# Attention of a graph layer: pairs of heads in plain float32 on halves of the array, two steps to a turn

## The chip, the cores and the metric

One core of one Trainium2 chip. The metric is the device time of one launch in microseconds (us). TensorE multiplies matrices, VectorE, ScalarE and GpSimd work on elements, SyncE (SP) issues most transfers. PSUM, which TensorE writes, has eight banks here, `bank[0]` to `bank[7]`, each of 128 partitions x 512 float32.

## The reference, cut to what matters

```python
xn = layernorm(x)                                   # 1250 x 512
neigh = segment_sum(xn[src], dst)                   # 40000 edges
rst = (1 + eps) * xn + neigh
gnn = relu(rst @ W1 + b1) @ W2 + b2 + xn            # hidden 1024
q, k, v = split(xn @ W_qkv.T)                       # 8 heads of 64
attn = relu((q * 64**-0.5) @ k.T) @ v               # per head, no softmax
x = x + gnn + attn @ W_out.T + b_out
x = x + moe(layernorm(x))                           # 16 experts, top 2, hidden 256
```

## The kernel before

All work is ordered by hand: each engine has its own list of instructions, and counting semaphores tie them together. One arena in SBUF holds nearly all tensors, which reuse each other's places.

The stages. (1) Layer norm of ten tiles of 128 nodes (the last has 98), turned by TensorE (L1058). (2) Projections k and q by pairs of heads (L1141), 24 groups, then v by tile of nodes (L1152), 10 groups; these 34 "turns" are `NPRE`. (3) Attention. (4) Output projection (L1203). (5) The hidden layer of the graph part (L1272) and its second product (L1218). (6) Routing and the expert loop.

Graph work goes beside (2) and (3). Instead of gathering rows, the kernel counts edges: for each window of 32 target nodes (`w`, 40 of them) VectorE makes pairs of one-hot matrices in float16 from 125 edges (L825, L827) in a ring of `RING` slots, and TensorE multiplies them (L1081), which gives the adjacency counts of the window in PSUM. ScalarE copies the window (L613). After each four windows (group `g`) TensorE multiplies the counts by xn, ten float32 matmuls of 512 columns (`neighbours`, L1110), VectorE adds (1 + eps) xn (L834), TensorE turns the sum (L1117), ScalarE saves it (L618). Where each piece goes is a table: `dve_after`, `pe_after`, `act_after` give for each turn or attention step what an engine does after it. `EVERY` is the number of steps from one window to the next, `start(w)` the step of window w. GpSimd picks the columns of each window's edges (L509, L510) no more than three windows ahead of what VectorE has made.

Attention before runs by single heads. A step is (head, block of 416 or 418 queries, tile of 128 keys): 8 x 3 x 10 = 240 steps. q and k are split into a high part in float32r and a rest, so that float32r products add up to float32 precision. GpSimd splits each head (`split_head`, L494 to L497) on the head's own 64 partitions, and three transfers (L369) copy the parts to the other 64, so that k's high part and rest lie one above the other (`k_hl`). A score tile is then two matmuls over 128 rows, with q's high part and with its rest (L1169). ScalarE makes relu and its float32r rounding `p_hi` (L657), VectorE the rest of it, `p_lo` (L861). v has high and low halves side by side (`v_hl`, L637 and L842), so a value product is again two matmuls (L1185, L1188); its two halves of output partitions are added by ScalarE and VectorE (L646, L854) into q's place. TensorE runs the scores two steps ahead: scores(s + 2), values(s), graph(s). `NQB` = 3 banks hold scores, banks 3 and 4 (`AV`) the values, banks 5 and 7 (`AW`) windows, bank 6 (`NB`) the sums.

v_hl lies over the place of the kept x. So x is fetched again after attention's last step, GpSimd adds xn (L562), and VectorE the biases (L874), before the output projection is added (L876). SP's list in this part: three transfers of a head, one fill of an eighth of the expert slots with zeros (L373), for each head; then w_o; after the last step x, w1, w2.

Of the kernel before, what the change touches and what calls it, by code (L numbers as in the profile page):

```python
# [47 lines left out]
RING = 6  # L48
# [20 lines left out]
def layer(nc, x, src, dst, wqkv, wo, bo, gw1, gb1, gw2, gb2, geps, rw, rb, ew, eb1, eb2, out):  # L69
# [8 lines left out]
    with ExitStack() as ctx:  # L78
# [34 lines left out]
        NPB = 4  # L113
        RSTB = RINGB + 6400
# [4 lines left out]
        zeros = at(RINGB + 10240, [D])  # L119
# [17 lines left out]
        k_hl = [split_tensor(f"k_hl{i}", b, [N]) for i, b in enumerate((SET0, SET1))]  # L137
        q_hi = [split_tensor(f"q_hi{i}", b + 4 * N, [N]) for i, b in enumerate((SET0, SET1))]
        q_lo = [split_tensor(f"q_lo{i}", b + 8 * N, [N]) for i, b in enumerate((SET0, SET1))]
        k_lo = split_tensor("k_lo", TMPK, [N])  # L140
        p_hi = split_tensor("p_hi", PROBS, [NPB, BW])
        p_lo = split_tensor("p_lo", PROBS + NPB * 4 * BW, [NPB, BW])
# [4 lines left out]
        v_hl = split_tensor("v_hl", VT, [NT, HEADS, 2, DH])  # L147
# [9 lines left out]
        def w2_hi(m):  # L157

            return v_hl[:, m // 2, 4 * (m % 2):4 * (m % 2) + 4, :, :].rearrange("p a b c -> p (a b c)")
# [21 lines left out]
        def small(k, *shape):  # L181
# [57 lines left out]
        NQB, AV, AW, NB = 3, 3, (5, 7), 6  # L239
# [4 lines left out]
        x_again = sem("x_again")  # L244
# [18 lines left out]
        qk_ps, p_hi_ready, p_lo_ready, av_step, av_half, av_saved = (  # L263
            sem(s) for s in ("qk_ps", "p_hi_ready", "p_lo_ready", "av_step", "av_half", "av_saved"))
        v_hi_ready, v_lo_ready = sem("v_hi_ready"), sem("v_lo_ready")
        head_split = sem("head_split")
        head_ready = [sem(f"head_ready{h}") for h in range(HEADS)]
# [33 lines left out]
        steps = [(h, b, t) for h in range(HEADS) for b in range(len(BLOCKS)) for t in range(NT)]  # L301
        NS = len(steps)
        SPH = len(BLOCKS) * NT
# [5 lines left out]
        EVERY = 6.7  # L309
        pe_after, act_after, dve_after = ([[] for _ in range(NPRE + NS)] for _ in range(3))  # L310

        def start(w):
            return FROM + w * (NPRE - FROM) / EARLY if w < EARLY else NPRE + (w - EARLY) * EVERY

        for w in range(NW):
            for k in range(USUAL[w]):
                made = int(start(w) + k * (start(w + 1) - start(w)) / USUAL[w])
                dve_after[made].append(("pair", w, k))


                if w % 2 == 0 and k == USUAL[w] - 1:
                    held = ("pair", w, k)
                elif w % 2 == 1 and k == 0:
                    pe_after[made + 1] += [("pair", w, k), ("spare", w - 1), held]
                    act_after[made + (2 if made + 2 < NPRE else 4)].append(("window", w - 1))
                else:
                    pe_after[made + 1].append(("pair", w, k))
            if w % 2 == 1:
                act_after[made + (2 if made + 2 < NPRE else 4)].append(("window", w))
# [11 lines left out]
        def _(sp):  # L341
# [23 lines left out]
            for h in range(HEADS):  # L365
                own, other = slice(DH * (h % 2), DH * (h % 2) + DH), slice(DH - DH * (h % 2), 2 * DH - DH * (h % 2))
# [3 lines left out]
                if h == 0:  # L370
                    sp.wait_ge(zeros_ready, 1)
                fill = FILLS[h]
# [3 lines left out]
            sp.wait_ge(qk_ps, SPH * (HEADS - 1))  # L376
            sp.dma_start(w_o[:, :, :], wo).then_inc(wo_in, 16)
# [48 lines left out]
        def _(pool):  # L426
# [57 lines left out]
            def split_head(h):  # L484

                p, own, i = h // 2, slice(DH * (h % 2), DH * (h % 2) + DH), h % 2
                pool.wait_ge(proj_saved, 6 * (p + 1))
                if h >= 1:
                    pool.wait_ge(head_ready[h - 1], 48)
                if h >= 2:  # L490
                    pool.wait_ge(qk_ps, SPH * (h - 1))
                if h == 1:
                    pool.wait_ge(proj_ps, NPROJ + NT)
                link(pool.tensor_copy(k_hl[i][own, :], k_t[own, p, 0:N]))  # L494
                link(pool.tensor_tensor(k_lo[own, :], k_t[own, p, 0:N], k_hl[i][own, :].bitcast(f32), ALU.subtract))
                link(pool.tensor_copy(q_hi[i][own, :], q_t[own, p, :]))
                link(pool.tensor_tensor(q_lo[i][own, :], q_t[own, p, :], q_hi[i][own, :].bitcast(f32), ALU.subtract))  # L497
                pool.sem_inc(head_split, 1)

# [52 lines left out]

            for _, what, i in sorted([(start(0) + 0.5 if h == 0 else NPRE + SPH * (h - 1) + 1, "head", h) for h in range(HEADS)]
                                     + [(start(max(w - 2, 0)), "cols", w) for w in range(NW)]
                                     + [(start(w), "spare", w) for w in range(0, NW, 2)]):
                {"head": split_head, "cols": window_columns, "spare": spare_chunks}[what](i)
# [34 lines left out]
        def _(act):  # L591
# [43 lines left out]
            for t in range(NT):  # L635
                act.wait_ge(proj_ps, NPROJ + t + 1)
                act.activation(v_hl[:, t, :, 0, :], bank[(NPROJ + t) % 5][:, :].rearrange("p (h d) -> p h d", h=HEADS),  # L637
                               copy).then_inc(v_hi_ready, 1)
                graph(NPROJ + t)

            def save_attention(m):

                h, b = m // 3, m % 3
                o, n = BLOCKS[b]
                act.wait_ge(av_step, NT * (m + 1))
                act.activation(q_t[DH * (h % 2):DH * (h % 2) + DH, h // 2, o:o + n], bank[AV + m % 2][0:DH, 0:n],  # L646
                               copy).then_inc(av_half, 1)

            for s, (h, b, t) in enumerate(steps):
# [5 lines left out]
                if s == 0:  # L655
                    act.wait_ge(proj_ps, NPRE)
                act.activation(p_hi[0:kt, s % NPB, 0:n], bank[s % NQB][0:kt, 0:n], ACT.Relu).then_inc(p_hi_ready, 1)  # L657
                if s > NT and s % NT == 1:
                    save_attention(s // NT - 1)
                graph(NPRE + s)  # L660
            save_attention(HEADS * 3 - 1)
# [9 lines left out]
            for f, tiles in enumerate(FC_TILES):  # L671
# [3 lines left out]
                for m in range(KH):  # L675
                    if tiles[0] == 0:
                        act.activation(w2_hi(m), w2[:, m, :], copy).then_inc(w2_hi_ready, 1)
# [46 lines left out]
        def _(dve):  # L724
# [113 lines left out]
            for turn in range(FROM, NPRE):  # L838
                if turn >= NPROJ:
                    t = turn - NPROJ  # L840
                    dve.wait_ge(v_hi_ready, t + 1)
                    dve.tensor_tensor(v_hl[:, t, :, 1, :],  # L842
                                      bank[turn % 5][:, :].rearrange("p (h d) -> p h d", h=HEADS),
                                      v_hl[:, t, :, 0, :].bitcast(f32), ALU.subtract).then_inc(v_lo_ready, 1)
# [3 lines left out]
            def add_attention(m):  # L848

                h, b = m // 3, m % 3  # L850
                o, n = BLOCKS[b]
                to = q_t[DH * (h % 2):DH * (h % 2) + DH, h // 2, o:o + n]
                dve.wait_ge(av_half, m + 1)
                dve.tensor_tensor(to, to, bank[AV + m % 2][DH:P, 0:n], ALU.add).then_inc(av_saved, 1)  # L854

            for s, (h, b, t) in enumerate(steps):
                n = BLOCKS[b][1]
                kt = rows(t)
                dve.wait_ge(p_hi_ready, s + 1)

                dve.scalar_tensor_tensor(out=p_lo[0:kt, s % NPB, 0:n], in0=bank[s % NQB][0:kt, 0:n], scalar=0.0,  # L861
# [519 lines left out]
```

## Time and profile before

| | us |
|---|---|
| median of 3 runs | 878.91 (877.94 to 879.23) |
| the profiled execution's own time | 879.67 |
| its span | 877.5 |
| PE busy in the span | 775.1 (88%) |
| DVE (VectorE) busy | 521.7 (59%) |
| ACT (ScalarE) busy | 281.1 (32%) |
| POOL (GpSimd) busy | 155.3 (18%) |

PE is TensorE's matmuls, PEld its weight loads. A record's duration runs until its result is out; records in a row begin before the last one ends, so the cost of a matmul in a row is the time from start to start. Each plain float32 matmul shows as two records, each with a load; a float32r or float16 one as one record. PEclk is the granted TensorE clock, 1.00 for 2.4 GHz and 0.50 for 1.2 GHz. Shapes in a row are partitions x elements.

### The profile page before, as it was taken

What the parts mean: (1) busy time and instruction counts of PE and PEld (TensorE: products, weight loads), DVE (VectorE), ACT (ScalarE), POOL (GpSimd) and SP (SyncE); (2) the same over time, 40 slices, a digit from 0 to 9 for tenths busy, and PEclk for the clock granted to TensorE, in tenths of its full rate; (3) what the DMA queues carried; (4) which work ended last, traced back from release to release, by engine and by line L of the source; (5) the groups of instructions that cost most, each with busy time, mean ns of one, the idle gap of its engine ahead of it and who ended that gap; (6) DMA issues with size and microseconds to landing.
All of it is one profiled execution on the core that took longest, in us unless ns stands there. A gap on an engine that the chain in (4) does not pass through costs nothing.

```text
span 877.5 us, 11469 instructions
## 1 busy us (share of the span) xinstructions
PE 775.1 (88%) x3351; PEld 517.9 (59%) x3352; DVE 521.7 (59%) x1494; ACT 281.1 (32%) x578; POOL 155.3 (18%) x198
## 2 busy tenths in 40 slices
PE   4999998989989998979799999999998599999910
PEld 2555443666756676656577744677887256766700
DVE  4563336798989989898877534435445523333234
ACT  2212111352534444343345402323333123434300
POOL 5040003022130403040400042002021100000045
PEclk9999999999999999999799999999999559999965
DMA  9126000807162526253351091001015945343357
GB/s 296 8 44 241 1 0 1 295 1 251 46 210 87 182 104 198 98 160 137 105 191 49 1 357 47 1 0 72 1 73 192 377 184 187 109 135 114 131 163 235
DMA packets 48071, 111.61 MB, mean 127 GB/s; under 512 B 7066, under 2 KB 7082, under 8 KB 45584
## 3 DMA queue, kind: packets, MB, share of 16 engines
q1 hardware_dynamic: 43248, 91.41, 30.8%
q0 software_dynamic: 3616, 11.17, 4.0%
q10 hardware_dynamic: 1152, 8.39, 2.4%
q8 instruction: 24, 0.39, 0.2%
q14 instruction: 31, 0.25, 0.1%
HBM read 44.73 MB, written 58.54 MB: 118 GB/s over the span
## 4 chain that ended last, share of the span: by engine, by line
PE 70%; DVE 20%; issue 4%; POOL 2%; DMA 2%; ACT 2%; SPq 0%; DVEq 0%; POOLq 0%
PE bank L1110 8%; PE bank L1141 7%; PE bank L1272 7%; DVE arena L825 6%; PE bank L1218 6%; PE bank L1333 6%; PE bank L1169 6%; DVE p_lo L861 6%; PE bank L1346 5%; PE bank L1081 4%; PE bank L1152 4%; PE bank L1203 4%; DVE arena L827 3%; PE bank L1188 3%; PE bank L1185 3%
## 5 line engine op out<-in xcount | busy, mean ns | idle before, releaser
L657 ACT ACTIVATE p_hi<-bank 128x416 fp32r<-128x416 f32 (+1 forms) x240 | 123.8, 518 | 201.2 <-PE bank L1169 199.7
L861 DVE SCALAR_TENSOR_TENSOR p_lo<-bank,p_hi 128x416 fp32r<-128x416 f32 (+1 forms) x240 | 140.2, 586 | 40.7 <-ACT p_hi L657 39.7
L825 DVE TENSOR_SCALAR arena<-iota,arena 125x128 f16<-125x128 f16 x392 | 137.9, 352 | 37.0 <-PE bank L1081 34.8
L827 DVE TENSOR_SCALAR arena<-iota,arena 125x320 f16<-125x320 f16 x392 | 115.7, 295 | 0.0
L1169 PE MATMUL bank<-q_hi,k_hl 128*128 128x416 f32 (+1 forms) x240 | 114.9, 479 | 0.1
L1188 PE MATMUL bank<-p_lo,v_hl 128*128 128x416 f32 (+1 forms) x240 | 91.0, 379 | 21.6 <-DVE p_lo L861 21.2
L1110 PE MATMUL bank<-arena 128*128 128x512 f32 x200 | 103.0, 597 | 0.8 <-ACT arena L618 0.8
L1081 PE MATMUL bank<-arena 125*128 125x320 f16 x392 | 96.7, 311 | 5.8 <-issue 3.5
L1185 PE MATMUL bank<-p_hi,v_hl 128*128 128x416 f32 (+1 forms) x240 | 86.5, 360 | 0.0
L1169 PE MATMUL bank<-q_lo,k_hl 128*128 128x416 f32 (+1 forms) x240 | 86.1, 359 | 0.0
L1081 PEld LDWEIGHTS bank<-arena 125*128 125x128 f16 x392 | 34.4, 100 | 75.7 <-issue 53.2
L1141 PE MATMUL bank<-arena 128*128 128x416 f32 (+1 forms) x192 | 73.1, 529 | 2.1 <-ACT arena L600 2.1
L1272 PE MATMUL bank<-arena 128*128 128x384 f32 (+2 forms) x256 | 70.3, 430 | 0.0
L1188 PEld LDWEIGHTS bank<-p_lo,v_hl 128*128 128x128 f32 x240 | 46.6, 194 | 35.2 <-DVE p_lo L861 34.1
L1333 PEld LDWEIGHTS bank<-arena 128*128 128x128 f32 x448 | 53.0, 198 | 17.4 <-issue 16.0
L1333 PE MATMUL bank<-arena 128*128 128x128 f32 x448 | 55.3, 283 | 6.6 <-issue 5.6
L1026 DVE COPY arena<-arena 128x1024 f32 x30 | 20.8, 695 | 67.3 <-issue 67.3
L1169 PEld LDWEIGHTS bank<-q_hi,k_hl 128*128 128x128 f32 x240 | 47.1, 196 | 20.2 <-issue 13.5
L1272 PEld LDWEIGHTS bank<-arena 128*128 128x128 f32 x256 | 47.7, 190 | 17.6 <-issue 0.5
L1141 PEld LDWEIGHTS bank<-arena 128*128 128x128 f32 x192 | 36.2, 195 | 29.7 <-issue 26.3
L509 POOL COPY arena<-arena 125x20 f32 (+1 forms) x40 | 8.5, 212 | 246.8 <-DVE arena L827 207.5
L1346 PE MATMUL bank<-arena 128*128 x112 | 50.4, 592 | 0.0
(208 smaller groups left out, 1018.9 us busy)
## 6 DMA issues: line engine op xcount, KB each, us to landing
slots<-arena SPq DMA_DIRECT2D x6, 5376.0 KB, 19.3
slots<-arena SPq DMA_DIRECT2D x2, 5120.0 KB, 19.0
arena<-in_ew SPq DMA_DIRECT2D x8, 1024.0 KB, 10.7
arena<-in_ew ACTq DMA_DIRECT2D x8, 1024.0 KB, 13.2
arena<-slots SPq DMA_DIRECT2D x32, 256.0 KB, 2.8
slots<-arena SPq DMA_DIRECT2D x28, 256.0 KB, 2.1
arena<-in_gw SPq DMA_DIRECT2D x2, 2048.0 KB, 16.7
arena<-in_wqkv SPq DMA_DIRECT2D x3, 1024.0 KB, 14.2
```

The lines of the kernel that those rows point to most:

```text
L657: act.activation(p_hi[0:kt, s % NPB, 0:n], bank[s % NQB][0:kt, 0:n], ACT.Relu).then_inc(p_hi_ready, 1)
L825: dve.tensor_scalar(ring[:, at_slot:at_slot + P], iota16[0:CE, 0:P], window_cols[:, i % WBUF, 1, k:k + 1], None, ALU.is_equal)
L827: dve.tensor_scalar(ring[:, at_slot + P:at_slot + OHW], iota16[0:CE, :], window_cols[:, i % WBUF, 0, k:k + 1], None, ALU.is_equal).then_in ...
L861: dve.scalar_tensor_tensor(out=p_lo[0:kt, s % NPB, 0:n], in0=bank[s % NQB][0:kt, 0:n], scalar=0.0, in1=p_hi[0:kt, s % NPB, 0:n].bitcast(f3 ...
L1081: return pe.matmul(bank[AW[w % 2]][:, 0:WCOL], of[:, at_slot:at_slot + P], of[:, at_slot + P:at_slot + OHW], start=start, stop=stop, skip_ ...
L1110: ins = pe.matmul(bank[NB][:, :], a_t[:, g % 2, t, :], xn[:, t, :], start=(t == 0), stop=(t == NT - 1))
L1141: ins = pe.matmul(bank[g % 5][:, 0:n], w_qkv[:, k, c:c + P], xn_t[:, k, o:o + n], start=(k == 0), stop=(k == KD - 1))
L1169: ins = pe.matmul(bank[s % NQB][0:kt, 0:n], k_hl[h % 2][:, t * P:t * P + kt], q[h % 2][:, o:o + n], start=first, stop=not first)
L1185: pe.matmul(bank[AV + m % 2][:, 0:n], v_hl[0:kt, t, h, :, :], p_hi[0:kt, s % NPB, 0:n], start=(t == 0), stop=False)
L1188: pe.matmul(bank[AV + m % 2][:, 0:n], v_hl[0:kt, t, h, :, :], p_lo[0:kt, s % NPB, 0:n], start=False, stop=(t == NT - 1)).then_inc(av_step, 1)
L1272: ins = pe.matmul(bank[g % 4][:, 0:n], w1[:, k, m * P:(m + 1) * P], rst_t[:, k, o:o + n], start=(k == 0), stop=(k == KD - 1))
L1333: ins = pe.matmul(bank[a][:, m * P:(m + 1) * P], w1_now[:, a, k * DFF + m * P:k * DFF + m * P + P], xg_t[:, a, k, :], start=(k == 0), stop ...
```

## The change

Attention runs by pairs of heads in plain float32. Nothing is split any more: head 2p lies on partitions 0 to 63 and head 2p + 1 on 64 to 127 of q_t and k_t as the projections leave them. A step is (pair, block, tile of keys), 120 in all. Its scores are two float32 matmuls of 64 rows, one on the upper and one on the lower half of the array's rows, into two banks. ScalarE makes relu of the first head, VectorE of the second, both in float32. Its values are two float32 matmuls over 128 rows, each on one half of the array's columns, into the two halves of one bank, which ScalarE saves in one copy. Two steps make a turn: TensorE does the scores of both, then the graph work of both, then the values of both. Probabilities have two buffers instead of four, values one bank instead of two. A window comes every 3.35 steps, a one-hot pair is used two steps after it is made, the ring has eight slots, and the sums go two to a step. v_sb has half of v_hl's size, so x stays where it is: it isn't fetched again, and GpSimd adds xn and the biases as soon as its list reaches them. w_o and w2 are fetched at attention's start.

```diff
-RING = 6
+RING = 8
-        NPB = 4
+        NPB = 2
+        probs = at(PROBS, [NPB, 2, BW])
-        v_hl = split_tensor("v_hl", VT, [NT, HEADS, 2, DH])
+        v_sb = at(VT, [NT, D])
+        w2_hi = split_tensor("w2_hi", VT, [KH, D])
-        NQB, AV, AW, NB = 3, 3, (5, 7), 6
+        AV, AW, NB = 4, (5, 7), 6
-        steps = [(h, b, t) for h in range(HEADS) for b in range(len(BLOCKS)) for t in range(NT)]
+        steps = [(p, b, t) for p in range(PAIRS) for b in range(len(BLOCKS)) for t in range(NT)]
-        EVERY = 6.7
+        EVERY = 3.35
+        def used(made):
+            return made + (2 if made >= NPRE - 1 else 1)
...
-                    pe_after[made + 5 + t].append(("sum", g, t))
-                dve_after[made + NT + 6].append(("sum", g))
-                pe_after[made + NT + 7].append(("turn", g))
-                act_after[made + NT + 10].append(("turn", g))
+                    pe_after[used(made) + 3 + t // 2].append(("sum", g, t))
+                dve_after[used(made) + 8].append(("sum", g))
+                pe_after[used(made) + 11].append(("turn", g))
+                act_after[used(made) + 12].append(("turn", g))
...
-            for h in range(HEADS):
...
-                sp.wait_ge(head_split, h + 1)
-                for to, of in ((k_hl[h % 2], k_lo), (q_hi[h % 2], q_hi[h % 2]), (q_lo[h % 2], q_lo[h % 2])):
-                    sp.dma_start(to[other, :].bitcast(f32), of[own, :].bitcast(f32)).then_inc(head_ready[h], 16)
+            sp.wait_ge(zeros_ready, 1)
+            for i, fill in enumerate(FILLS):
+                sp.wait_ge(qk_ps, 1 + i * NS // len(FILLS))
...
+                if i == 0:
+                    sp.dma_start(w_o[:, :, :], wo).then_inc(wo_in, 16)
+                    sp.dma_start(w2[:, :, :], gw2).then_inc(w2_in, 16)
...
             sp.wait_ge(av_step, NS)
-            sp.dma_start(xr[:, 0:9, :], xv).then_inc(x_again, 16)
-            sp.wait_ge(xpad_ready, 2)
-            sp.dma_start(xr[0:LAST, NT - 1, :], x[(NT - 1) * P:N, :]).then_inc(x_again, 16)
             sp.dma_start(w1[:, :, :], gw1).then_inc(w1_in, 16)
-            sp.dma_start(w2[:, :, :], gw2).then_inc(w2_in, 16)
...
-            def split_head(h):
...
-            pool.wait_ge(av_step, NS)
-            link(pool.memset(xr[96:P, NT - 1, :], 0.0))
-            pool.sem_inc(xpad_ready, 1)
-            pool.wait_ge(x_again, 32)
             for t in range(NT):
                 link(pool.tensor_tensor(xr[:, t, :], xr[:, t, :], xn[:, t, :], ALU.add))
+                link(pool.tensor_tensor(xr[:, t, :], xr[:, t, :], bias_b2[:, :], ALU.add))
                 pool.sem_inc(base_ready, 1)
...
+                act.activation(v_sb[:, t, :], bank[(NPROJ + t) % 5][:, :], copy).then_inc(v_saved, 1)
...
+                act.activation(q_t[:, p, o:o + n], bank[AV][:, 0:n], copy).then_inc(av_saved, 1)
...
+                if s >= NT and t == 0:
+                    save_attention(s // NT - 1)
                 act.wait_ge(qk_ps, s + 1)
                 if s >= NPB:
                     act.wait_ge(av_step, s - NPB + 1)
...
+                act.activation(probs[0:kt, s % NPB, 0, 0:n], bank[2 * (s % 2)][0:kt, 0:n],
+                               ACT.Relu).then_inc(p0_ready, 1)
+                if s % 2 == 1:
+                    graph(NPRE + s - 1)
+                    graph(NPRE + s)
...
+                dve.wait_ge(qk_ps, s + 1)
+                if s >= NPB:
+                    dve.wait_ge(av_step, s - NPB + 1)
+                dve.tensor_single_scalar(probs[0:kt, s % NPB, 1, 0:n], bank[2 * (s % 2) + 1][0:kt, 0:n], 0.0,
+                                         op=ALU.max).then_inc(p1_ready, 1)
+                if s % 2 == 1:
+                    for what in dve_after[NPRE + s - 1] + dve_after[NPRE + s]:
+                        do(*what)
...
-                link(dve.tensor_tensor(xr[:, t, :], xr[:, t, :], bias_b2[:, :], ALU.add))
...
             def scores(s):
...
+                if s >= 2:
+                    pe.wait_ge(p0_ready, s - 1)
+                    pe.wait_ge(p1_ready, s - 1)
+                for a in range(2):
+                    ins = pe.matmul(bank[2 * (s % 2) + a][0:kt, 0:n], k_t[DH * a:DH * a + DH, p, t * P:t * P + kt],
+                                    q_t[DH * a:DH * a + DH, p, o:o + n], start=True, stop=True,
+                                    tile_position=(DH * a, 0))
                 ins.then_inc(qk_ps, 1)
+            def values(s):
...
+                if t == 0 and m >= 1:
+                    pe.wait_ge(av_saved, m)
+                pe.wait_ge(p0_ready, s + 1)
+                pe.wait_ge(p1_ready, s + 1)
+                for a in range(2):
+                    h = 2 * p + a
+                    ins = pe.matmul(bank[AV][DH * a:DH * a + DH, 0:n], v_sb[0:kt, t, h * DH:h * DH + DH],
+                                    probs[0:kt, s % NPB, a, 0:n], start=(t == 0), stop=(t == NT - 1),
+                                    tile_position=(0, DH * a), skip_group_check=True)
+                ins.then_inc(av_step, 1)
+
+            for s in range(0, NS, 2):
+                scores(s)
+                scores(s + 1)
                 graph(NPRE + s)
+                graph(NPRE + s + 1)
+                values(s)
+                values(s + 1)
```

## Rows read from the trace of the kernel before

**Rows 1.** By stretch: length, busy PE, PEld, DVE, ACT, POOL, PEclk, DMA share, GB/s.
```profile
146.20:505.00 358.80, 330.81 (x1498) 234.88 (x1499) 307.20 (x904) 149.62 (x306) 70.62 (x86) 0.97 0.39 129
696.00:714.00 18.00, 17.14 (x24) 5.14 (x25) 5.82 (x10) 1.70 (x7) 0.00 (x0) 0.50 0.56 229
```
**Rows 2.** The chain of waits around attention: start us, us, what.
```profile
141.41 3.45 PE bank L1152 x8
...
504.99 34.33 PE bank L1203 x80
539.32 20.64 PE bank L1272 x64
```
**Rows 3.** The chain inside attention, with sums and then without.
```profile
212.64 0.86 PE bank L1110 x2
...
213.64 0.38 PE bank L1169 x2
...
214.21 0.19 PE bank L1188
...
222.54 0.17 DVE arena L825
222.70 0.21 DVE arena L827
222.91 0.50 DVE p_lo L861
```
**Rows 4.** Busy PE and PEld in attention's stretch: L1110, then L1081, then L1117.
```profile
146.20:505.00 358.80, 93.84 (x182) 34.46 (x182) 0.97 0.39 129
146.20:505.00 358.80, 81.94 (x315) 26.96 (x315) 0.97 0.39 129
146.20:505.00 358.80, 5.99 (x40) 4.98 (x40) 0.97 0.39 129
```
**Rows 5.** The chain where eight float32 and two one-hot records follow each other.
```profile
70.46 2.81 PE bank L1141 x8
...
218.93 0.27 PE bank L1081 x2
```
**Rows 6.** Waits in attention's stretch: us in total, times, longest.
```profile
PE bank L1188 <- DVE p_lo L861: 21.2, 17, 3.5
```
**Rows 7.** GpSimd's passes and L825: timeline rows, durations min/median/max, groups.
```profile
245.03 2.88 POOL L497 TENSOR_TENSOR q_lo<-arena,q_hi 64x1250 fp32r<-64x1250 f32 x1
245.63 2.33 DVE L825 TENSOR_SCALAR arena<-iota,arena 125x128 f16<-125x128 f16 x1
...
L825 DVE TENSOR_SCALAR arena<-iota,arena x392: 234/246/2847, 48.1 to 472.4; 125x128 f16<-125x128 f16 x196
...
L495 POOL TENSOR_TENSOR k_lo<-arena,k_hl 64x1250 fp32r<-64x1250 f32 x8 | 23.0, 2880 | 0.7
...
L562 POOL TENSOR_TENSOR arena<-arena 128x512 f32<-128x512 f32 x10 | 16.3, 1634 | 11.8 <-DMA arena<-in_x 10.2 <-POOL arena L562 1.6
```
**Rows 8.** TensorE's timeline from products with 16 rows to turns onto 16 columns.
```profile
701.32 0.33 PEld L1309 LDWEIGHTS bank<-b_sb,arena 16*128 16x128 f32 x1 [0.52 <-issue]
...
703.03 1.91 PE L1309 MATMUL bank<-b_sb,arena 16*128 16x512 f32 x2
704.86 0.10 PEld L1303 LDWEIGHTS bank<-ident,arena 128*16 128x16 f32 x2 [1.50 <-issue]
```
**Rows 9.** Timeline in attention: a first record after a wait, and following ones.
```profile
249.10 0.46 PE L1188 MATMUL bank<-p_lo,v_hl 128*128 128x418 f32 x1 [0.90 <-DVE p_lo L861]
...
246.05 0.35 PE L1169 MATMUL bank<-q_lo,k_hl 128*128 128x418 f32 x1
246.05 0.19 PEld L1185 LDWEIGHTS bank<-p_hi,v_hl 128*128 128x128 f32 x1
```
**Rows 10.** TensorE's timeline where attention begins.
```profile
145.54 0.57 PE L1081 MATMUL bank<-arena 125*128 125x320 f16 x3
146.26 0.19 PEld L1169 LDWEIGHTS bank<-q_hi,k_hl 128*128 128x128 f32 x1 [0.48 <-DVE v_hl L842]
```

More of the change, by code:

```diff
@@ L262, in layer @@
         neigh_ps, rst_ready, rstt_ps, rstt_saved = (sem(s) for s in ("neigh_ps", "rst_ready", "rstt_ps", "rstt_saved"))
[L263 to L267, printed above, removed]
+        qk_ps, p0_ready, p1_ready, av_step, av_saved = (
+            sem(s) for s in ("qk_ps", "p0_ready", "p1_ready", "av_step", "av_saved"))
+        v_saved = sem("v_saved")
         out_ps, out_added = sem("out_ps"), sem("out_added")
@@ L323, in layer @@
                 elif w % 2 == 1 and k == 0:
-                    pe_after[made + 1] += [("pair", w, k), ("spare", w - 1), held]
-                    act_after[made + (2 if made + 2 < NPRE else 4)].append(("window", w - 1))
+                    pe_after[used(made)] += [("pair", w, k), ("spare", w - 1), held]
+                    act_after[used(made) + 1].append(("window", w - 1))
                 else:
-                    pe_after[made + 1].append(("pair", w, k))
+                    pe_after[used(made)].append(("pair", w, k))
             if w % 2 == 1:
-                act_after[made + (2 if made + 2 < NPRE else 4)].append(("window", w))
+                act_after[used(made) + 1].append(("window", w))
             if w % WPG == WPG - 1:
@@ L551, in spare_window @@
                     pool.sem_inc(spare_waited, 1)
-            for _, what, i in sorted([(start(0) + 0.5 if h == 0 else NPRE + SPH * (h - 1) + 1, "head", h) for h in range(HEADS)]
-                                     + [(start(max(w - 2, 0)), "cols", w) for w in range(NW)]
+            for _, what, i in sorted([(start(max(w - 2, 0)), "cols", w) for w in range(NW)]
                                      + [(start(w), "spare", w) for w in range(0, NW, 2)]):
-                {"head": split_head, "cols": window_columns, "spare": spare_chunks}[what](i)
-            pool.wait_ge(av_step, NS)
-            link(pool.memset(xr[96:P, NT - 1, :], 0.0))
-            pool.sem_inc(xpad_ready, 1)
-            pool.wait_ge(x_again, 32)
+                {"cols": window_columns, "spare": spare_chunks}[what](i)
             for t in range(NT):
                 link(pool.tensor_tensor(xr[:, t, :], xr[:, t, :], xn[:, t, :], ALU.add))
+                link(pool.tensor_tensor(xr[:, t, :], xr[:, t, :], bias_b2[:, :], ALU.add))
                 pool.sem_inc(base_ready, 1)
@@ L654, in _ @@
                     act.wait_ge(av_step, s - NPB + 1)
[L655 to L661, printed above, removed]
+                act.activation(probs[0:kt, s % NPB, 0, 0:n], bank[2 * (s % 2)][0:kt, 0:n],
[3 more added lines that the diff above has]
+                    graph(NPRE + s)
+            save_attention(NM - 1)
             def exponents(f):
@@ L676, in _ @@
                     if tiles[0] == 0:
-                        act.activation(w2_hi(m), w2[:, m, :], copy).then_inc(w2_hi_ready, 1)
+                        act.activation(w2_hi[:, m, :], w2[:, m, :], copy).then_inc(w2_hi_ready, 1)
                     act.wait_ge(hid_ps, g + 1)
@@ L838, in _ @@
             for turn in range(FROM, NPRE):
[L839 to L844, printed above, removed]
                 for what in dve_after[turn]:
                     do(*what)
[L848 to L856, printed above, removed]
+            for s, (p, b, t) in enumerate(steps):
                 n = BLOCKS[b][1]
                 kt = rows(t)
-                dve.wait_ge(p_hi_ready, s + 1)
-                dve.scalar_tensor_tensor(out=p_lo[0:kt, s % NPB, 0:n], in0=bank[s % NQB][0:kt, 0:n], scalar=0.0,
-                                         in1=p_hi[0:kt, s % NPB, 0:n].bitcast(f32), op0=ALU.max,
-                                         op1=ALU.subtract).then_inc(p_lo_ready, 1)
-                if s > NT and s % NT == 2:
-                    add_attention(s // NT - 1)
-                for what in dve_after[NPRE + s]:
-                    do(*what)
-            add_attention(HEADS * 3 - 1)
+                dve.wait_ge(qk_ps, s + 1)
[6 more added lines that the diff above has]
+                        do(*what)
             for t in range(NT):
@@ L1155, in _ @@
                 graph(NPROJ + t)
-            pe.wait_ge(v_lo_ready, NT)
+            pe.wait_ge(v_saved, NT)
             def scores(s):
-                h, b, t = steps[s]
+                p, b, t = steps[s]
                 o, n = BLOCKS[b]
                 kt = rows(t)
-                if s >= NQB:
-                    pe.wait_ge(p_lo_ready, s - NQB + 1)
-                if s % SPH == 0:
-                    pe.wait_ge(head_split, h + 1)
-                    pe.wait_ge(head_ready[h], 48)
-                for first, q in ((True, q_hi), (False, q_lo)):
-                    ins = pe.matmul(bank[s % NQB][0:kt, 0:n], k_hl[h % 2][:, t * P:t * P + kt], q[h % 2][:, o:o + n],
-                                    start=first, stop=not first)
-                ins.then_inc(qk_ps, 1)
-            scores(0)
-            scores(1)
-            for s, (h, b, t) in enumerate(steps):
-                if s + 2 < NS:
-                    scores(s + 2)
+                if s >= 2:
[5 more added lines that the diff above has]
+                                    tile_position=(DH * a, 0))
+                ins.then_inc(qk_ps, 1)
+            def values(s):
+                p, b, t = steps[s]
                 n = BLOCKS[b][1]
@@ L1180, in _ @@
                 m = s // NT
-                if t == 0 and m >= 2:
-                    pe.wait_ge(av_saved, m - 1)
-                pe.wait_ge(p_hi_ready, s + 1)
-                pe.matmul(bank[AV + m % 2][:, 0:n], v_hl[0:kt, t, h, :, :], p_hi[0:kt, s % NPB, 0:n],
-                          start=(t == 0), stop=False)
-                pe.wait_ge(p_lo_ready, s + 1)
-                pe.matmul(bank[AV + m % 2][:, 0:n], v_hl[0:kt, t, h, :, :], p_lo[0:kt, s % NPB, 0:n],
-                          start=False, stop=(t == NT - 1)).then_inc(av_step, 1)
+                if t == 0 and m >= 1:
[11 more added lines that the diff above has]
+                scores(s + 1)
                 graph(NPRE + s)
+                graph(NPRE + s + 1)
+                values(s)
+                values(s + 1)
             pe.wait_ge(wo_in, 16)
@@ L1196, in _ @@
                 r = rows(t)
-                pe.wait_ge(av_saved, SPH * HEADS // NT - len(BLOCKS)
-                           + sum(1 for o, n in BLOCKS if o < t * P + r))
+                pe.wait_ge(av_saved, NM - len(BLOCKS) + sum(1 for o, n in BLOCKS if o < t * P + r))
                 if t >= 8:
@@ L1216, in mix @@
                         pe.wait_ge(hid_lo, hidden + m + 1)
[L1217 removed]
+                    for i, (h, w) in enumerate(((h_hi, w2_hi[:, m, :]), (h_lo, w2_hi[:, m, :]), (h_hi, w2_lo[:, m, :]))):
                         ins = pe.matmul(bank[4 + t % 2][0:r, :], h[:, m, c:c + r], w,
```

47 lines of the change are left out of this document (7 added, 40 removed).

## The prediction

> **What bounds the kernel now.** Start with the busy time by stretch [rows 1]: attention, woven with most of the graph work, is the stretch from 146.2 to 505.0 us, 358.8 of the span's 877.5 us. TensorE and VectorE are both near full there (331 and 307 us busy), ScalarE and GpSimd are not. The chain of waits [rows 2] shows what ends last around it: V's projections in front and the output projection behind are dense TensorE work, as 34.33 us from 504.99 and the next line from 539.32 on. So the change is decided inside the stretch.
>
> Inside it, the chain [rows 3] alternates. Where a step carries sums of neighbours it is pure TensorE work: from 212.64 on the chain is two records of L1110 (0.86 us), a one-hot product, and the four fp32r matmuls, 0.38 for the scores' two and 0.19 for each value product. Between the sums the chain goes through VectorE: p_lo 0.50 us, one-hots 0.17 and 0.21.
>
> What TensorE must do there, by start-to-start times rather than by record durations, which overlap: the sums are 182 records [rows 4], and the output projection's 80 records of 512 columns take 34.33 us [rows 2], 0.43 each, so 78.3 us. One-hot products: 315 records [rows 4] at 0.137 (two take 0.27 us [rows 5]), 43.2. Turns of the sums: 40 [rows 4] of 128 columns, at the float32 rate of [rows 5] (2.81 us for 8 x 418 columns) 0.11 each, 4.4. Graph work is 125.9 us. Attention is 960 records of fp32r at 0.188, 180.5. Together 306.4; the other 52.4 us are lost. The granted clock of 0.97 over the stretch means 3% of 359 us, 11 us, at twice that length of half clock; the remaining 41 are waits, mostly for VectorE: TensorE stood 21.2 us before L1188 for p_lo [rows 6], and what longer records hide is not in that. One cause of the late VectorE is visible: a one-hot of L825 lasts 0.25 us in the median and up to 2.85, and the long one in the timeline lies under a GpSimd pass of the head split and ends with it [rows 7]. GpSimd is busy 70.6 us in the stretch [rows 1], most of it with them (L495 alone 23.0 [rows 7]).
>
> **What the change does, part by part.** I count per turn of two steps, 60 turns.
>
> *Matmuls of attention.* Removed: 180.5 us. Added: per step two scores and two value products in plain float32. A plain float32 matmul is two records, and eight records of 418 columns take 2.81 us [rows 5], 0.35 each. So a turn has 8 score records and 8 value records. If nothing runs beside anything: 16 x 0.35 x 60 = 336 us, the upper end. If the halves run side by side perfectly: 168 us, the lower end. No row of this trace shows two matmuls on different halves. I take a staggered overlap: records start in the order of the program (as in all rows here), the two records of one half use the same cells and follow each other, and only the second record of half 0 can lie beside the first of half 1. Eight records then take five slots: 5 x 0.35 = 1.75 us for scores and as much for values, 3.5 per turn, 210 us. That is nearer the lower end; I choose it because the halves share neither rows, bank nor partitions (scores), or columns and partitions (values).
>
> The Trainium skill, "TensorE: Matmul & The Clock Gate", Part 3, holds that matmuls on different parts of the array start some 4 ns apart. No row here shows it; by it with both records side by side the sum would be the lower end, which is in the third rival.
>
> *Going between shapes.* TensorE now goes rows-halved (scores), whole (graph), columns-halved (values), rows-halved again: three changes a turn, 180 in all. The nearest rows are products with 16 rows followed by turns onto 16 columns [rows 8]. Within the run of L1309 a load (701.32) starts while the matmul before it runs. The L1303 load at 704.86 starts only when the last L1309 record, which began about 703.88 (703.03 + 1.91 less its length of 1.06), has streamed its 0.85 us: 0.13 us later, though nothing else held it. At full clock half of that. Then the load itself is exposed: a first record after a wait lasts 0.46 us against 0.35 of a following one [rows 3, 9], 0.11 us. I take 0.2 us a change: 36 us. Below: nothing, if loads go on ahead as they do between fp32r and float32 here. Above: 0.35 (tail of 0.16, load of 0.19), 63 us.
>
> The page "TensorEngine Tiling (Array Packing)", Key Properties, of the Trainium skill says that changing the tiling mode drains the engine. By this rule, the trace agrees: the late load of [rows 8]. It speaks against this change: without it the sum would be 36 us less.
>
> *VectorE and GpSimd.* p_lo (240 x 0.50) becomes 120 reliefs of half 1; add_attention and the lower half of V go; the head splits go, with their DMAs and waits. Per turn VectorE then has 2 x 0.50 (no row shows this operation; L861 of the same shape is the nearest, 0.58 at most) and some 5.9 pairs of one-hots (a window's 392/40 = 9.8 pairs [rows 7] per 3.35 steps) at 0.38, 3.2 us. A turn without sums holds TensorE for 3.5 + 0.6 + 0.8 = 4.9 us, so VectorE is no longer late. The ring of 8 lets one turn's pairs be made while the last turn's are used. ScalarE has half its reliefs. The graph work between scores and values covers both reliefs (0.5 us each); if that cover is gone, in the turns with little of it, at most 0.6 us a turn.
> What comes back: GpSimd's base adds, now 20 passes, are no longer behind attention's end. They start when the last window's columns are done, about step 100 of 120, and last some 20 x 1.63 = 33 us [rows 7]. They can hold L825 as the split did, in the last three windows: before, 70.6 us of GpSimd work went with at most 41 us of waiting; in proportion 19, less because TensorE's turns are longer: 8 us. Clock loss: 4 us instead of 11, since fewer gaps go before it. So 12 us for what is left of 52.4.
>
> *One AV bank.* The first values of a block wait for ScalarE's save of the last. Behind that wait stand values and the next scores, but two scores and the graph work are ahead of it, longer than the 0.52 us copy: nothing. Without this cover 11 x 0.7 = 8 us.
>
> *Order of DMAs, around the stretch.* The fills now wait on scores, w_o and w2 go in early, x isn't fetched again, VectorE's L874 adds go to GpSimd. Nothing of this is on the path: L1203 and L1272 follow attention without a gap [rows 2]; w1 now starts at attention's end and has 34 us. The first scores waited for V's lower half (their load stood 0.48 us [rows 10]); of this the stream of the last one-hot product, three from 145.54 at 0.137, hides all but 0.3 us: -0.3 us.
>
> **Sum.** Stretch after: 125.9 + 210 + 36 + 12 = 383.9 us, against 358.8: +25.1. With -0.3: +24.8. The profiled execution took 879.67 us (its span and 2.2 us around it), so 904.5; the median, 878.91, is 0.8 lower, so by it 903.7: forecast 904 us. Own range 879 to 932 (changes at 0.06 to 0.35 us; the upper end leaves no room for more waits).
>
> **Rivals.**
> *No overlap.* Float32 records on halves run one after another. For: no row shows overlap. Against: the halves share nothing. 336 instead of 210: +126, 1030 us.
> *Overlap held back by loads.* A half's weights are loaded only once the record before it has started, as each load here does [rows 3, 9]. Then a pair of score matmuls takes 0.35 + 0.19 + 0.35 + 0.19 = 1.08 us, and a value pair with 64-column loads (0.14, between 0.10 for 16 columns and 0.19 for 128 [rows 8, 9]) 0.98: 4.12 a turn, 247 us, +37: 941 us.
> *Faster: the changes of shape cost little.* Place: the three borders of each turn. The stretch breaks even where attention's part of a turn is (358.8 + 0.3 - 125.9 - 12)/60 = 3.69 us; five slots twice are 3.5, so below 0.06 us a change the kernel is faster. At nothing: 210 + 125.9 + 12 = 347.9, which is 10.9 less, 868 us. Complete overlap with changes at 0.2 is 168 + 36: 862 us; both, 826. For it: fp32r, float32 and float16 follow each other here without a gap. Against: [rows 8]. I price it at 865.
> *Half clock.* If halves don't keep the granted clock up, TensorE's part of the stretch doubles: 372 more, 1276 us. In 696 to 714 us TensorE is busy with 16-row products at clock 0.50 [rows 1]; but the whole-array work behind it starts at that clock too, so this speaks little for it.
>
> **How the numbers follow.** Staggered overlap 0.38; held by loads 0.14; no overlap 0.26; faster 0.19; half clock 0.03. A difference under 0.2% is what a measurement can't tell from none. The third rival and a thin edge of the forecast give faster 0.20, same 0.04, slower 0.76. The range 850 to 1035 takes in all but half clock, double luck, and no overlap with dearer changes.
>
> **What would show it.** L1110 and L1081 keep their counts. The score and value lines show 480 records each; the chain through a turn gives the slots: 1.75 us for four score matmuls is the forecast, 2.8 no overlap, 1.4 full. At each border the first load starts after the last matmul's stream, or not. VectorE's share falls to about 60%, its L825 is long only near the end. Wrong would be: attention's part of a turn under 3.7 or over 4.5 us, or TensorE waiting for reliefs by more than 10 us in all.

## The result: faster, 848.4 us against 878.4

| | us |
|---|---|
| changed kernel, median of 4 | 848.41 (845.18 to 849.28) |
| kernel before, median of 4 | 878.42 (877.84 to 879.23) |
| ratio, 95% interval | 0.9651 (0.9624 to 0.9678) |
| profiled executions | 848.35 (span 846.6) against 879.67 (877.5) |

The forecast was 904, its range 850 to 1035: wrong in sign, and the result lies just under the range.

The chain of waits of the changed kernel, around attention and in two turns of it (columns as in [rows 2]):

```profile
146.44 1.67 PE bank L1113 x8
...
203.64 1.72 PE bank L1056 x4
205.36 0.41 PE bank L1027 x3
205.77 1.55 PE bank L1130 x8
207.32 1.60 PE bank L1113 x8
208.91 1.91 PE bank L1056 x4
210.83 0.82 PE bank L1027 x6
211.64 1.55 PE bank L1130 x8
213.19 1.60 PE bank L1113 x8
214.79 0.92 PE bank L1027 x6
...
474.07 34.53 PE bank L1152 x80
```

L1113 are the scores, L1130 the values, L1056 the sums (L1110 before), L1027 the one-hot products (L1081), L1152 the output projection (L1203). That projection begins at 474.07 instead of 504.99 [rows 2]: 30.9 us earlier, and the span is 30.9 us shorter. All of the gain is in attention's stretch. There the chain is TensorE alone from attention's start to 404 us, so that VectorE's pieces between the sums [rows 3] are gone; from 404 to 435 us it runs mostly through VectorE's one-hots, which the run late_adds explains below. The stretch by engine (columns as in [rows 1]):

```profile
146.40:474.10 327.70, 323.33 (x1492) 133.43 (x1492) 214.18 (x753) 84.83 (x174) 40.20 (x76) 1.00 0.39 144
```

The granted clock is 1.00 where it was 0.97, VectorE has 214 us of work where it had 307. Eight score records take 1.60 us up to the next work. At 0.35 us a record, eight one after another would be 2.8, and the forecast's five slots 1.75; four slots are 1.40, and the 0.20 left is the border. The timeline shows why: records come in pairs that start within 0.01 us of each other, and so do their loads. The two loads of a pair take 0.14 us together, and the trace has 0.13 to 0.14 for each of them (the first row holds two such pairs, 0.05 us apart):

```profile
205.70 0.20 PEld L1130 LDWEIGHTS bank<-arena 128*64 128x64 f32 x4 [0.26 <-issue]
205.70 1.27 PE L1130 MATMUL bank<-arena 128*64 128x416 f32 x6
...
206.10 0.14 PEld L1130 LDWEIGHTS bank<-arena 128*64 128x64 f32 x2 [0.21 <-issue]
206.45 0.14 PEld L1130 LDWEIGHTS bank<-arena 128*64 128x64 f32 x2 [0.21 <-issue]
```

Six value records last 1.27 us in all, from the first's start to the last's end: three pairs.

What TensorE waits for in the stretch (line, us in total, times, longest) is 4.3 us, against 21.2 for p_lo alone before [rows 6] (L789 and L791 make the two one-hots of a pair, L812 are VectorE's reliefs, L602 is ScalarE's save of V):

```profile
PE bank L1027 <- DVE arena L791: 2.6, 4, 1.1
PE bank L1130 <- DVE arena L812: 1.1, 4, 0.3
PE bank L1027 <- issue: 0.3, 1, 0.3
PE bank L1113 <- ACT arena L602: 0.3, 1, 0.3
```

### The profile page after: what moved, and what is told of

Its sections match the earlier page's. It is cut to its first block, busy times and chain, and to the rows that moved or that the text cites. A ratio compares the mean times of both kernels' runs of the same rounds, so it can differ in the third digit from the quotient of the medians.

```text
span 846.6 us, 11316 instructions
## 1 busy us (share of the span) xinstructions
PE 768.3 (91%) x3351; PEld 417.3 (49%) x3352; DVE 411.5 (49%) x1330; ACT 216.1 (26%) x446; POOL 98.8 (12%) x175
## 4 chain that ended last, share of the span: by engine, by line
PE 84%; DVE 5%; issue 3%; DMA 2%; POOL 2%; SPq 1%; ACT 1%; DVEq 0%; POOLq 0%
PE bank L1113 11%; PE bank L1130 10%; PE bank L1056 10%; PE bank L1087 7%; PE bank L1221 7%; PE bank L1167 7%; PE bank L1282 7%; PE bank L1027 6%; PE bank L1295 6%; PE bank L1098 4%; PE bank L1152 4%; POOL arena L550 2%; PE bank L1258 2%; DMA arena<-in_x 2%; PE bank L1264 1%
## 5 line engine op out<-in xcount | busy, mean ns | idle before, releaser
L789 DVE TENSOR_SCALAR arena<-iota,arena 125x128 f16<-125x128 f16 x392 | 115.9, 296 | 93.2 <-PE bank L1027 91.2
L791 DVE TENSOR_SCALAR arena<-iota,arena 125x320 f16<-125x320 f16 x392 | 117.2, 299 | 0.0
L620 ACT ACTIVATE arena<-bank 128x416 f32<-128x416 f32 (+1 forms) x120 | 62.2, 518 | 200.4 <-PE bank L1113 200.4
L812 DVE TENSOR_SCALAR arena<-bank 128x416 f32<-128x416 f32 (+1 forms) x120 | 70.6, 591 | 80.7 <-PE bank L1113 74.9
L1113 PE MATMUL bank<-arena 64*128 64x416 f32 (+1 forms) x480 | 100.2, 535 | 0.3 <-ACT arena L602 0.3
L1130 PE MATMUL bank<-arena 128*64 128x416 f32 (+1 forms) x480 | 97.2, 525 | 1.3 <-DVE arena L812 1.1
L1056 PE MATMUL bank<-arena 128*128 128x512 f32 x200 | 96.2, 605 | 0.0
L1027 PE MATMUL bank<-arena 125*128 125x320 f16 x392 | 71.2, 300 | 3.0 <-DVE arena L791 2.6
L1113 PEld LDWEIGHTS bank<-arena 64*128 64x128 f32 x480 | 40.6, 183 | 58.2 <-issue 57.6
L1027 PEld LDWEIGHTS bank<-arena 125*128 125x128 f16 x392 | 35.9, 97 | 63.4 <-issue 44.3
L1282 PEld LDWEIGHTS bank<-arena 128*128 128x128 f32 x448 | 53.3, 199 | 17.4 <-issue 15.7
L1221 PEld LDWEIGHTS bank<-arena 128*128 128x128 f32 x256 | 47.7, 190 | 17.6 <-issue 0.5
L1056 PEld LDWEIGHTS bank<-arena 128*128 128x128 f32 x200 | 34.9, 189 | 42.6 <-issue 41.9
L1130 PEld LDWEIGHTS bank<-arena 128*64 128x64 f32 x480 | 29.4, 136 | 43.5 <-issue 36.7
L1087 PEld LDWEIGHTS bank<-arena 128*128 128x128 f32 x192 | 35.7, 193 | 29.9 <-issue 25.4
L534 POOL DMA_INDIRECT slots<-arena,slot x20 | 19.9, 996 | 208.9 <-DVEq L872 204.0
```

What stands on the lines that cost most here:

```text
L620: act.activation(probs[0:kt, s % NPB, 0, 0:n], bank[2 * (s % 2)][0:kt, 0:n], ACT.Relu).then_inc(p0_ready, 1)
L789: dve.tensor_scalar(ring[:, at_slot:at_slot + P], iota16[0:CE, 0:P], window_cols[:, i % WBUF, 1, k:k + 1], None, ALU.is_equal)
L791: dve.tensor_scalar(ring[:, at_slot + P:at_slot + OHW], iota16[0:CE, :], window_cols[:, i % WBUF, 0, k:k + 1], None, ALU.is_equal).then_in ...
L812: dve.tensor_single_scalar(probs[0:kt, s % NPB, 1, 0:n], bank[2 * (s % 2) + 1][0:kt, 0:n], 0.0, op=ALU.max).then_inc(p1_ready, 1)
L1027: return pe.matmul(bank[AW[w % 2]][:, 0:WCOL], of[:, at_slot:at_slot + P], of[:, at_slot + P:at_slot + OHW], start=start, stop=stop, skip_ ...
L1056: ins = pe.matmul(bank[NB][:, :], a_t[:, g % 2, t, :], xn[:, t, :], start=(t == 0), stop=(t == NT - 1))
```

## The experiments

Theory after the result: records on the two halves run side by side in full (168 us of slots); the three changes of shape a turn cost nearly what was forecast; and the larger part of the gain is what the old form lost in waits and half clock, 52.4 us of its stretch. Where a kernel leaves values out, the router sends the rows elsewhere, and the expert loop of 8.5 us a round runs 15 times (one_half) or 13 times (b_no_split, b_both) instead of 14: so I compare where the output projection begins, and give that beside the time. It begins at 505.0 before and 474.1 in the changed kernel.

### One half of the rows for both heads

```diff
-  k_t[DH * a:DH * a + DH, ...], q_t[DH * a:DH * a + DH, ...], tile_position=(DH * a, 0)
+  k_t[0:DH, ...], q_t[0:DH, ...], tile_position=(0, 0)
```

> The changed kernel with both heads' scores on the lower half of the array's rows (head 2p's k and q are used for both heads, so head 2p+1's scores are left out); everything else the same. Theory (records of different halves run side by side, each as long as a whole-array record of as many columns): eight score records a turn take eight slots of 0.35 us instead of four, 60 x 4 x 0.35 = +84 us against the changed kernel's 848, so about 932. Rival (a record on half the array is simply cheap, and side by side explains nothing): no change, 848. Rival (staggered as forecast): from five slots to eight, +63, 911.

Measured 938.6 us (ratio to before 1.068, 1.067 to 1.070); the output projection begins at 555.68, +81.6. The chain:

```profile
203.98 2.99 PE bank L1113 x8
```

2.99 instead of 1.60 for the same eight records: eight slots (2.80) and the same 0.19 at the border. A record on half the array is as long as one on the whole, and the other half is free beside it. Both rivals fall: they expected nothing, and 63 us.

### The two matmuls of one half next to each other

```diff
-                scores(s)
-                scores(s + 1)
+                scores(s, (0,))
+                scores(s + 1, (0,))
+                scores(s, (1,))
+                scores(s + 1, (1,))
```

> The changed kernel with the four score matmuls of a turn in another order: head 2p of both steps, then head 2p+1 of both steps, so that in the program's order the two matmuls of one half stand next to each other. If a record can only start beside its neighbour in the program (strict order of starts), then of four records on one half and four on the other one pair overlaps: seven slots instead of four, +63 us, about 911. If the engine takes whichever half is free, 848 as the changed kernel.

TensorE's wait for the reliefs stands ahead of each step's first matmul, and the semaphore that tells of a step's scores is raised by its second.

Measured 852.0 us (ratio to before 0.969, 0.968 to 0.971), 3.6 over the changed kernel. The chain of this kernel has the same score block:

```profile
208.29 1.60 PE bank L1113 x8
209.89 1.92 PE bank L1056 x4
```

So program order does not set the pairs: TensorE takes the next record of each half, over at least one matmul of the other. The staggered overlap of the forecast assumed the opposite.

The semaphore keeps the order of the program all the same. VectorE's reliefs of one turn in the changed kernel, whose scores begin at 207.25, and of the same turn here, where they begin at 208.22:

```profile
208.26 1.29 DVE L812 TENSOR_SCALAR arena<-bank 128x416 f32<-128x416 f32 x2 [1.89 <-PE bank L1113]
...
209.93 1.09 DVE L812 TENSOR_SCALAR arena<-bank 128x416 f32<-128x416 f32 x2 [2.59 <-PE bank L1113]
```

The first relief starts 1.01 us after the scores in the changed kernel and 1.71 us after them here: the first step is told of only when both steps' matmuls are done (in the median turn the semaphore rises at 1.69 and 1.73 us, against 0.99 and 1.69). Where little or no graph work covers the reliefs, TensorE waits for them: its waits for L812 are 2.6 us instead of 1.1, and the two turns without graph work are 0.70 us longer each. Compared turn by turn with the changed kernel, the turns with such a wait are 2.6 us longer in all. What is left of the 3.6 us lies mostly in the time of the base adds (406 to 431 us), where this trace has one piece of 3.4 us at half clock; its cause is not shown.

### Whole-array matmuls in their place

```diff
-                for a in range(2):
-                    ins = pe.matmul(bank[2 * (s % 2) + a][0:kt, 0:n], k_t[DH * a:DH * a + DH, ...], tile_position=(DH * a, 0))
+                for a in ((1, 0) if s < 2 else (0,)):
+                    ins = pe.matmul(bank[2 * (s % 2) + a][0:kt, 0:n], k_t[:, p, ...], q_t[:, p, o:o + n], ...)
...
+                pe.matmul(bank[AV][:, 0:n], v_sb[0:kt, t, 2 * p * DH:2 * p * DH + P], probs[0:kt, s % NPB, 0, 0:n], ...)
```

> The changed kernel with each pair of half-array matmuls replaced by one whole-array matmul of the same columns (both heads' rows summed in one score product, both heads' v columns against head 2p's probabilities; the values of the two heads are not kept apart). It has four slots of 0.35 us for scores and four for values a turn, as two halves side by side would, but no change of shape. Theory (three changes a turn at 0.09 us of gap and 0.05 to 0.10 of exposed load, 0.54 us a turn): 32 us less than the changed kernel, about 816. Rival (the changes are hidden behind other waits): within 5 us of 848.

Measured 823.6 us (ratio 0.938, 0.936 to 0.939), the projection begins at 448.85: -25.2. Its blocks:

```profile
201.05 1.40 PE bank L1127 x4
202.45 1.40 PE bank L1113 x4
...
203.84 1.72 PE bank L1056 x4
...
209.17 0.82 PE bank L1027 x6
```

1.40 instead of 1.55 for values (L1127 here) and 1.60 for scores: exactly four slots, with nothing at the borders. The graph work behind the scores is shorter too, 1.72 instead of 1.91 where it begins with sums and 0.82 instead of 0.92 where it begins with one-hot products. By these rows a turn's three changes cost 0.45 to 0.54 us, as expected, which is 27 to 32 us in 60 turns. 25.2 us over 180 changes would be 0.14 each, but this kernel's gain falls short for two reasons: it does the scores of the first two steps twice (1.5 us), and TensorE waits longer in it for the one-hots under GpSimd's base adds (its waits in the stretch are 6.5 us instead of 4.3). In the trace of late_adds below, where TensorE waits for 0.3 us in all, the 60 score blocks take 96.4 us and the 60 value blocks 93.0, where 1.40 each would be 168.0 together; with 0.10 to 0.20 at the first graph record of 58 turns (8.5) the changes cost 30 us, 0.17 each.

### Turns of four steps

```diff
-RING = 8
+RING = 20
-        NPB = 2
+        NPB = 4
-        EVERY = 3.35
+        EVERY = 3.2
+        TURN = 4
-                    sp.dma_start(w2[:, :, :], gw2).then_inc(w2_in, 16)
...
+            sp.dma_start(w2[:, :, :], gw2).then_inc(w2_in, 16)
...
+            for s in range(0, NS, TURN):
+                for i in range(TURN):
+                    scores(s + i)
+                for i in range(TURN):
+                    graph(NPRE + s + i)
+                for i in range(TURN):
+                    values(s + i)
```

> The changed kernel with turns of four steps (scores of four, graph work, values of four), four buffers of probabilities, a ring of 20 one-hot slots, w2 fetched after attention. 90 changes of shape instead of 180: -16 us. Third scores of a turn wait for the first's relief, 0.15 us a turn: +4.5. Where a block begins in mid-turn its first values wait for ScalarE's save: 6 x 0.65 = +4. Theory: about 841. Rival (VectorE, with 13 pairs of one-hots in a row behind four reliefs, is late): 848 or more.

A window comes every 3.2 steps here instead of 3.35.

Measured 861.8 us (ratio 0.982, 0.980 to 0.983): slower than turns of two. The chain of a turn (L1142 are the values, L1125 the scores), and the wait that stands out:

```profile
210.16 2.94 PE bank L1142 x16
213.10 1.60 PE bank L1125 x8
214.70 0.09 issue
214.79 1.67 PE bank L1125 x8
...
PE bank L1125 <- DVE arena L823: 12.5, 2, 11.4
```

Values gain 0.16 us (2.94 for 2 x 1.55), scores lose as much (3.36 for 2 x 1.60): the third step's scores wait 0.09 us for the first's relief and show their load again. Only the border at the graph work is saved. So the 16 us expected of fewer changes were not there; I had priced the wait and not the load behind it. And one wait of 11.4 us came in the time of GpSimd's base adds, with a clock of 0.89 from 415 to 460 us. In the changed kernel the same place looks like this:

```profile
423.98 1.31 POOL L527 TENSOR_TENSOR arena<-arena,bias_b 128x512 f32<-128x512 f32 x1
424.08 1.25 DVE L789 TENSOR_SCALAR arena<-iota,arena 125x128 f16<-125x128 f16 x1
425.26 0.29 DVE L791 TENSOR_SCALAR arena<-iota,arena 125x320 f16<-125x320 f16 x1
```

A one-hot that starts after a GpSimd pass ends with it (424.08 + 1.25 is 425.33, 423.98 + 1.31 is 425.29); the 17 of L789 that last over 1 us in the stretch all end 0.05 us after a pass. The reliefs, which read PSUM, are not held: L812 lasts 575 to 595 ns in all 120, and 575 to 582 in the six that start under an add. The Trainium skill, "SBUF — State Buffer", section "SBUF: two separate sides", says that VectorE and GpSimd share one pair of ports that one of them locks for its whole instruction. The trace agrees for the one-hots; on the reliefs it shows no hold.

### The base adds put off, with turns of two and of four

```diff
+            pool.wait_ge(onehots_ready, FIRST[NW])
             for t in range(NT):
                 link(pool.tensor_tensor(xr[:, t, :], xr[:, t, :], xn[:, t, :], ALU.add))
```

> The changed kernel with GpSimd's 20 base adds put off until the last one-hot pair is made. In the changed kernel TensorE waits some 5 us in 408 to 440 us for one-hots of 1.3 us each that lie under these adds. Theory: -5 us, about 843. Rival (TensorE's waits there are made up later, or the adds now come late for the output projection's banks): within 2 us of 848, or slower.

> The kernel with turns of four steps, and GpSimd's base adds put off until the last one-hot pair is made. That kernel took 862 us, with one wait of TensorE for VectorE of 11.4 us, and half clock for some 10 us behind it, in the time of the adds. Theory (the adds alone made it slower than turns of two): 862 - 11.4 - 5 = about 845, with late_adds at 843. Rival (13 pairs in a row are too many for VectorE anyway): above 852.

With turns of two: 842.8 us (ratio to before 0.960, 0.958 to 0.962), the best of all that keep the computation; the projection begins at 467.76, 6.3 us earlier, and the mean of the L789 group goes from 296 to 248 ns. With turns of four: 847.6 (0.966, 0.964 to 0.968), 14.2 less than four_steps, where turns of two gained 5.6; so the adds had cost that kernel 8.6 of its 13.4 us over turns of two. It stays 4.8 over them, not 2. Block by block in the two traces, scores take 6.8 us more than in turns of two (4.6 for the load shown again, the rest in two turns where TensorE waits for reliefs), values 0.5 more (4.6 saved at the borders, but 3.7 us of waits in mid-turn for ScalarE's save, expected as 4, and the loads behind them), and graph work 1.7 less.

### The kernel before without its waits

Head splits of 16 columns (b_no_split), p_lo of 64 columns (b_light), both (b_both):

```diff
+                c = N if h < 2 else 16
-                link(pool.tensor_copy(k_hl[i][own, :], k_t[own, p, 0:N]))
+                link(pool.tensor_copy(k_hl[i][own, 0:c], k_t[own, p, 0:c]))
...
+                c = n if s < NT * NPB else 64
-                dve.scalar_tensor_tensor(out=p_lo[0:kt, s % NPB, 0:n], in0=bank[s % NQB][0:kt, 0:n], scalar=0.0,
+                dve.scalar_tensor_tensor(out=p_lo[0:kt, s % NPB, 0:c], in0=bank[s % NQB][0:kt, 0:c], scalar=0.0,
```

> The kernel before with GpSimd's four passes of a head split cut to 16 columns for heads 2 to 7 (these heads run on what heads 0 and 1 left); transfers, waits and all other work stay. Of the 52.4 us that attention's stretch lost before, 41 were waits. Theory A (GpSimd's passes hold VectorE's one-hots, and TensorE waits for the late p_lo): -25 us or more, about 850. Theory B (VectorE simply has more to do than TensorE in steps without sums): at most -8, 871 or more.

> The kernel before with p_lo made for 64 of 416 columns after the first 40 steps (the other columns of the rest are left as they were), head splits as before: VectorE has some 200 x 0.37 = 73 us less to do in attention. Theory A (GpSimd's hold): at most -10 us, 869 or more. Theory B (amount of VectorE's work): -20 us or more, 858 or less.

> The kernel before with splits of 16 columns for heads 2 to 7 and p_lo made for 64 of 416 columns after the first 40 steps (the rest is left as it was). If the lost 52.4 us (waits for VectorE, and the half clock that follows them) are all that the new form took back, and fp32r matmuls at 0.188 us cost 180.5 us against 168 + 27 for halves with their changes of shape, this kernel comes to 879 - 45 = about 834 or less, under the changed kernel's 848. If the new matmuls themselves are the gain, it stays above 848.

Times: 844.5, 864.2 and 831.3 us (ratios 0.962, 0.984, 0.947; intervals 0.960 to 0.964, 0.983 to 0.986, 0.945 to 0.949), the first and the last with one round of experts fewer. The stretches, from 146.3 on, in that order:

```profile
146.30:477.50 331.20, 319.61 (x1491) 229.38 (x1492) 275.67 (x901) 148.40 (x304) 25.20 (x85) 0.99 0.42 140
...
146.30:491.60 345.30, 325.54 (x1497) 235.76 (x1496) 246.08 (x901) 149.50 (x306) 69.56 (x85) 0.96 0.40 134
...
146.30:465.20 318.90, 313.57 (x1494) 229.28 (x1493) 211.76 (x901) 149.09 (x307) 25.45 (x85) 0.99 0.44 146
```

Against 358.8 [rows 1]: -27.6 without the passes, -13.5 with less p_lo, -39.9 with both. Neither theory alone holds: A's bound for b_light (at most 10) and B's for b_no_split (at most 8) are both passed, and the two nearly add up (41.1). TensorE's wait for p_lo, 21.2 us before [rows 6], is in the same order:

```profile
PE bank L1189 <- DVE p_lo L862: 5.3, 6, 3.5
...
PE bank L1189 <- DVE p_lo L862: 17.9, 10, 3.5
...
PE bank L1190 <- DVE p_lo L863: 3.5, 1, 3.5
```

Without the passes VectorE has the same instructions and is busy 275.7 us instead of 307.2, and the mean of the L825 group falls from 352 to 273 ns: it was held. GpSimd's hold was some two thirds of the 39.9. With both gone the old fp32r form takes 318.9 us, 8.8 less than the new form's 327.7 and 2.9 less than the new form with late adds (321.8): the new matmuls are not the gain. They cost more on TensorE (168 + 30 against 180.5 us), and buy the end of the splits and of p_lo. With the missing round of experts (8.5 us) put back, b_both is near 840 us: over the 834 expected, as the waits were not all gone (3.5 us for p_lo), and still under the changed kernel's 848.

## Why the prediction was wrong

The sum, term by term, for the stretch (forecast 383.9, measured 327.7):

- *Graph work*, 125.9: right. In the changed kernel's stretch 180 sum records at 0.43, 315 one-hot products at 0.137 and 36 turns at 0.11 make 124.5.
- *Matmuls of attention*, 210: **the step that failed.** "Only the second record of half 0 can lie beside the first of half 1" is false; the halves run side by side in full, 168 us, -42. I had that end as the lower bound (168), put it into the third rival only, and gave that rival 0.19. The reason given, "records start in the order of the program", rested on rows in which all matmuls use the whole array, and so could not speak on halves at all; here the first record of half 1 starts within 0.01 us of the first of half 0, ahead of that half's second.
- *Going between shapes*, 36: the mechanism was right, the size a little high. The first load after a border starts late and shows. It is 30 us by the blocks of late_adds; the whole-array kernel's 25.2 is too low.
- *What is left of 52.4 us lost*, 12: about 6 by late_adds (the stretch is 5.9 us shorter: 321.8 from 146.0), all of it the base adds, foreseen at 8; the 4 for the clock did not come, its granted clock is 1.00 throughout. The terms as measured, 124.5 + 168 + 30 + 5.9, make 328.4, 0.7 over the stretch.
- *The rest of the kernel*, nothing: right. The output projection and all behind it take 372.5 us in both. The 0.3 us at attention's start did not come: it begins at 146.4, 0.2 later.

"Held by loads" fell with the first timeline: two loads start together. The third rival, "complete overlap with changes at 0.2", gave 862 with my 12 us of waits; it was the nearest case, and is 14 off, mostly by the waits and the changes (6 each). The prediction gave full overlap no chance of its own. The break-even of 3.69 us a turn stands: measured are 1.60 + 1.55 = 3.15, and 0.10 to 0.19 at the first graph record. The prediction named "attention's part of a turn under 3.7" as what would make it wrong.

## What to carry to other kernels

Two float32 matmuls on disjoint halves of the array cost one; price that as full overlap, plus about 0.17 us for each change of shape (0.10 to 0.20, by what comes first behind it), and group work by shape until a wait for PSUM costs as much as the change it saves (here turns of four steps gave nothing over turns of two). When a form of the computation needs help from GpSimd, price the hold on VectorE with it: here the end of that hold (27.6 us by b_no_split), not less work on TensorE, was most of what the change won, and moving twenty adds out of the way gave 5.6 us more.

## What the runs showed of the hardware

Records for different halves pair up although the program has two matmuls of one half in front of those of the other (1.60 us in both orders). Weight loads of the two halves also run together: two 64-column loads 0.14 us, as one. A matmul that runs ahead of one of the other half still reports in the order of the program: in apart the first step's semaphore rises 1.69 us after the first score record, when all four matmuls are done, and not at 0.99.
